# Stacking rotary tiles through a DRAM scratch, thin column tiles for small matmuls, and new engine orders between the MLP and the adapters of an adaLN block

## The chip, the cores and the metric

The kernel runs on one core of a Trainium2 chip. The metric is the device time of one execution in microseconds, as the median of several runs.

## The reference

The block takes x of 4 batch entries ("rows" below) by 512 positions by 256 features, all float32, and a condition vector for each row from which shifts, scales and gates are made.

```python
h = _layernorm(x) * (1 + ca) + sa
x = x + ga * attn_block(h)          # 32 heads of 8, rotary q and k, causal inside 4 blocks of 128,
                                    # RMS norms, then a gated MLP of 512 hidden features
h = _layernorm(x) * (1 + cb) + sb
x = x + gb * ffn_block(h)
# ffn_block: base = silu(h Wg) * (h Wu) @ Wd with 704 hidden features; a router over 8 experts
# (softmax, top 2) weights low-rank adapters of rank 16 on Wg, Wu and Wd, scaled by 2
```

Rotary positions: `x * cos + rot(x) * sin`. Accuracy near float32 is needed.

## The kernel before

Features lie on the 128 partitions and the 512 positions of a row along the free dimension. The four rows are worked one after another in a loop (three turns of `row_steps` and one last copy of it). Each engine runs its own list, written by hand, and waits on semaphores that count the steps of the others. Projections that need accuracy are made of three matmuls on a high and a low part of each operand (`product`, L1259 to L1261); the high part is a rounded copy made on ScalarE, the low part is the difference, made on VectorE.

A row runs through these stages: attention in eight units (2 halves of the heads by 4 blocks), output projection, MLP, then the front of the next row (`front_projections`) woven together with the second norm (`rest`) of this row, then router, adapters and feed-forward. The order of the front on the tensor engine (`front_projections`, L1328 on) is: four q/k projections (`project_qk`), the swap matmuls of the rotary step (`swap`, L1303), the mean and the mean of squares of `rest` (L1276, L1285), the spread of its reciprocal deviation (L1293) and the v projection (`project_v`, L1323 to L1325). Then come the router logits (L1501), the adapters' inner products `ag` and `au`, `base(0)`, transposed picks (L1537), `base(1)`, two more picks, `lora(0, 1)`, `down(0, 0)` and `lora(0, 2)` (L1565 to L1567).

Rotary tiles are four: 0 and 1 are q and k of the first half of the heads, 2 and 3 those of the second. For each tile ScalarE copies the projection out of PSUM (`copy_qk`, L666), GpSimd multiplies it by the cosine (`rope_cos`, L496, into the one buffer `q_cos`, so that it waits for the addition of the tile before), VectorE multiplies the swapped tile by the sine and adds (`rope_sin` L955, `rope_add` L961), ScalarE makes the high part (`rope_high`, L670) and VectorE the low part (`rope_low`, L966). The tile is then stacked: `stack_tile` (L378 to L392) copies three parts of four groups of 32 partitions into `q_st` or `k_st`, 12 DMAs a tile, SBUF to SBUF; SyncE issues tiles 0 to 2, GpSimd tile 3. `highs_back` (L442) copies the high parts into `q_high` and `k_high`, which are the buffers `n_hi` and `n_lo` of the projections, so it waits until those are read; that is four DMAs a tile.

Ahead of the loop SyncE runs `stack(0, 0)`, waits for the v projection and runs `highs_back`. GpSimd's `first_units` then spreads keys (`spread_keys`, L510), after waits for all weight chunks (`chunk_lo`), the rotary low parts and the keys' high parts. The weight chunks are split by ScalarE (`chunk_highs`, L631) and VectorE (`chunk_lows`, L906); three of six are split ahead of the first front and three behind it.

At the start of the feed-forward ScalarE runs `gate_silu(0)`, `copy_pick(0)`, `copy_pick(1)` (L805), and then the high parts of the adapters' inputs (L820); VectorE makes the picks (L1147 to L1156), `ff_product(0)` (L1191), `lora_input` (L1163) and `lora_low` (L1168). `product_high` (L801) writes into the buffers of the rotary high and low parts, so it waits for `half_stacked`.

Of the kernel before, what the change touches and what calls it, by code (L numbers as in the profile page):

```python
# [32 lines left out]
P = 128  # L33
# [122 lines left out]
def adaln_kernel(nc, x, smalls, wmod, wsplit, wplain, consts, masks, out):  # L156
    with ExitStack() as ctx:
# [41 lines left out]
        pool_mark = sb("pool_mark", [P, 1])  # L199
# [30 lines left out]
        qk_sb, q_cos, roped = tile_f[:, 0:2, :], tile_f[:, 2, :], tile_f[:, 4:6, :]  # L230
# [11 lines left out]
        lora_tmp = [tile_f[:, i, :] for i in (4, 6, 10, 11)]  # L242
# [40 lines left out]
        stacked = [signal(f"stacked{i}", PARTS * GQ * 16) for i in range(4)]  # L283
        v_proj = signal("v_proj", 2)
        v_copied = signal("v_copied", 2)
        high_back = [signal(f"high_back{i}", GQ * 16) for i in range(4)]
# [87 lines left out]
        def half_stacked(engine, row, half, ahead):  # L374

            for i in (2 * half, 2 * half + 1):
                engine.wait_ge(stacked[i].sem, stacked[i].count(row, PARTS * GQ * 16, ahead))

        def stack_tile(engine, row, i, ahead):

            half, is_k = i // 2, i % 2
            engine.wait_ge(rope_hi.sem, rope_hi.count(row, i + 1, ahead))
            engine.wait_ge(rope_lo.sem, rope_lo.count(row, i + 1, ahead))
            if engine is nc.gpsimd:

                nc.gpsimd.tensor_tensor(pool_mark[:], con("one"), con("one"), ALU.mult)
            hi, lo = rope_hl[i]
            dest = k_st if is_k else q_st
            for part, src in enumerate((hi, lo, hi) if is_k else (hi, hi, lo)):
                for gq in range(GQ):  # L390
                    engine.dma_start(dest[32 * part:32 * part + 32, half * GQ + gq, :].bitcast(F32),  # L391
                                     src[32 * gq:32 * gq + 32, :].bitcast(F32)).then_inc(stacked[i].sem, 16)  # L392
# [5 lines left out]
        def _(sp):  # L398
# [30 lines left out]
            def stack(row, ahead):  # L429
                for i in range(3):  # L430
                    stack_tile(sp, row, i, ahead)

            def highs_back(i, row, ahead):

                half, is_k = i // 2, i % 2
                dest, stack_of = (k_high, k_st) if is_k else (q_high, q_st)
                for gq in range(GQ):
                    if ahead:
                        src = stack_of[0:32, half * GQ + gq, :]
                    else:  # L440
                        src = rope_hl[i][0][32 * gq:32 * gq + 32, :]
                    sp.dma_start(dest[32 * gq:32 * gq + 32, half, :].bitcast(F32), src.bitcast(F32))\  # L442
                        .then_inc(high_back[i].sem, 16)

            def row_steps(row, last):
# [6 lines left out]
                half_stacked(sp, row, 1, 0)  # L452
                sp.wait_ge(high_back[2].sem, high_back[2].count(row, GQ * 16))
                load(x_res, row, res_loaded)
                if not last:
                    stack(row, 1)

                    for half in range(2):
                        half_stacked(sp, row, half, 1)
# [8 lines left out]
            stack(0, 0)  # L468
            sp.wait_ge(v_proj.sem, v_proj.count(0, 2))
            for i in range(4):  # L470
                sp.wait_ge(rope_hi.sem, rope_hi.count(0, i + 1))
                highs_back(i, 0, 0)
            with sp.Fori(0, B - 1) as row:
                row_steps(row, False)
# [5 lines left out]
        def _(pool):  # L480
# [9 lines left out]
            def rope_cos(row, i, ahead):  # L490

                pool.wait_ge(qk_copied.sem, qk_copied.count(row, i + 1, ahead))
                if i:

                    pool.wait_ge(rope_done.sem, rope_done.count(row, i, ahead))
                nc.gpsimd.tensor_tensor(q_cos, qk_sb[:, i % 2, :], con("cos"), ALU.mult).then_inc(cos_done.sem, 1)  # L496

            def spread_keys(row, u, ahead):

                blk, half = u % BLOCKS, u // BLOCKS  # L500
                if u in (0, BLOCKS):

                    tile = high_back[2 * half + 1]
                    pool.wait_ge(tile.sem, tile.count(row, GQ * 16, ahead))
# [55 lines left out]
            def row_steps(row, last):  # L560
# [21 lines left out]
                if not last:  # L582
                    rope_cos(row, 0, 1)
# [1154 lines left out]
```

## Time and profile before

| | |
|---|---|
| median of 3 runs | 754.75 us (754.65 to 755.93) |
| the profiled execution | 749.13 us |
| its span on the engines | 747.3 us |
| PE busy | 649.1 us (87%) |
| DVE, ACT, POOL busy | 410.6, 321.7, 224.9 us |
| start-up, until the first score matmul | 77.36 us |

In the profile PE is the tensor engine's matmuls and PEld its weight loads, DVE is VectorE, ACT ScalarE, POOL GpSimd and SP SyncE; a q behind the name is the engine's queue, which issues DMAs. L12 is line 12 of the kernel. "Idle before" is the time for which the engine stood before a group, with what released it.

### The profile page before, as it was taken

What the parts mean: (1) busy time and instruction counts of PE and PEld (TensorE: products, weight loads), DVE (VectorE), ACT (ScalarE), POOL (GpSimd) and SP (SyncE); (2) the same over time, 40 slices, a digit from 0 to 9 for tenths busy, and PEclk for the clock granted to TensorE, in tenths of its full rate; (3) what the DMA queues carried; (4) which work ended last, traced back from release to release, by engine and by line L of the source; (5) the groups of instructions that cost most, each with busy time, mean ns of one, the idle gap of its engine ahead of it and who ended that gap; (6) DMA issues with size and microseconds to landing.
All of it is one profiled execution on the core that took longest, in us unless ns stands there. A gap on an engine that the chain in (4) does not pass through costs nothing.

```text
span 747.3 us, 12089 instructions
## 1 busy us (share of the span) xinstructions
PE 649.1 (87%) x4536; PEld 441.6 (59%) x4536; DVE 410.6 (55%) x617; ACT 321.7 (43%) x472; POOL 224.9 (30%) x292
## 2 busy tenths in 40 slices
PE   3770799899999899999999899999999899868996
PEld 2750355667785466657785466657785466637673
DVE  1553456367746564368646564368646564436544
ACT  3332245636544246526534246525533444414442
POOL 3023576204201476115001476115001674010000
PEclk9995799999999899999998799999999899977998
DMA  8245120002302100003202110003202100000000
GB/s 334 71 144 144 33 59 1 2 0 72 99 1 56 61 28 2 1 0 98 72 1 57 51 36 2 1 1 96 73 1 56 57 2 2 1 0 1 0 1 28
DMA packets 16466, 32.62 MB, mean 44 GB/s; under 512 B 5280, under 2 KB 5920, under 8 KB 16160
## 3 DMA queue, kind: packets, MB, share of 16 engines
q1 hardware_dynamic: 14880, 28.74, 12.8%
q0 software_dynamic: 1536, 3.15, 1.5%
q8 instruction: 40, 0.66, 0.4%
q14 instruction: 10, 0.08, 0.0%
HBM read 12.99 MB, written 2.10 MB: 20 GB/s over the span
## 4 chain that ended last, share of the span: by engine, by line
PE 64%; issue 13%; DVE 8%; ACT 7%; SPq 4%; POOL 2%; DMA 1%; DVEq 0%; POOLq 0%; ACTq 0%
PE bank L1424 7%; PE bank L1359 7%; PE bank L1259 7%; PE bank L1260 6%; PE bank L1261 6%; PE bank L1376 3%; PE bank L1402 3%; SPq L391 3%; PE bank L1565 3%; PE bank L1567 3%; PE bank L1566 2%; PE bank L1386 2%; PE bank L1456 2%; ACT tile_f L735 2%; ACT arena L636 2%
## 5 line engine op out<-in xcount | busy, mean ns | idle before, releaser
L1000 DVE TENSOR_REDUCE arena<-bank 128x8 f32<-128x1024 f32 x64 | 77.9, 1223 | 80.8 <-PE bank L1376 80.6
L1359 PE MATMUL bank<-mask 128*128 128x512 bf16 x256 | 83.5, 410 | 29.5 <-POOL k_wide L510 26.2
L1191 DVE TENSOR_TENSOR arena<-arena,bank 128x512 f32<-128x512 f32 (+1 forms) x72 | 49.1, 687 | 82.1 <-ACT arena L785 81.6
L1259 PE MATMUL bank<-n_hi,w_lo 128*128 128x512 f32 x200 | 86.4, 432 | 8.4 <-DVE n_lo L1055 6.0
L785 ACT ACTIVATE arena<-bank 128x512 f32<-128x512 f32 (+1 forms) x72 | 42.5, 596 | 102.1 <-PE bank L1567 53.5
L1260 PE MATMUL bank<-n_lo,w_hi 128*128 128x512 f32 x200 | 80.3, 401 | 0.0
L1261 PE MATMUL bank<-n_hi,w_hi 128*128 128x512 f32 x200 | 80.1, 401 | 0.0
L510 POOL TENSOR_TENSOR k_wide<-n_lo,head_of 128x512 fp32r<-128x512 f32 x32 | 33.1, 1039 | 153.1 <-PE bank L1567 139.4
L735 ACT ACTIVATE tile_f<-bank 128x1024 f32<-128x1024 f32 x64 | 64.2, 1023 | 33.5 <-PE bank L1402 33.4
L719 ACT CAST q_st<-bank 4x512 fp32r<-4x512 f32 x32 | 18.5, 579 | 115.4 <-PE bank L1386 115.4
L530 POOL TENSOR_SCALAR arena_r<-q_st,const 100x512 fp32r<-100x512 f32 x96 | 64.9, 693 | 0.2
L1424 PE MATMUL bank<-tile_f,v_ex 128*32 128x128 f32 x1024 | 52.9, 275 | 2.5 <-ACT tile_f L735 2.5
L1402 PE MATMUL bank<-arena_r,k_st 100*128 100x512 f32 x128 | 54.5, 508 | 0.0
L1176 DVE TENSOR_TENSOR arena_r<-arena,arena_r 128x512 fp32r<-128x512 f32 (+1 forms) x72 | 52.0, 725 | 4.0 <-ACT arena_r L801 3.2
L1359 PEld LDWEIGHTS bank<-mask 128*128 128x128 bf16 x256 | 18.1, 103 | 59.5 <-issue 52.9
L1424 PE MATMUL bank<-tile_f,ones_ex 128*32 128x128 f32 x1024 | 52.3, 273 | 0.0
L1259 PEld LDWEIGHTS bank<-n_hi,w_lo 128*128 128x128 f32 x200 | 38.5, 193 | 22.8 <-DVE n_lo L1055 10.5
L1021 DVE RECIPROCAL arena<-bank 128x128 f32<-128x128 f32 x32 | 30.6, 957 | 37.0 <-PE bank L1424 37.0
L527 POOL TENSOR_TENSOR arena_r<-q_st,const 100x512 fp32r<-100x512 f32 x32 | 33.3, 1041 | 53.4 <-ACT q_st L719 53.4
L801 ACT CAST arena_r<-arena 128x512 fp32r<-128x512 f32 (+1 forms) x72 | 44.1, 613 | 7.5 <-PE bank L1261 4.8
L1260 PEld LDWEIGHTS bank<-n_lo,w_hi 128*128 128x128 f32 x200 | 38.6, 193 | 9.6 <-issue 1.9
L1261 PEld LDWEIGHTS bank<-n_hi,w_hi 128*128 128x128 f32 x200 | 38.4, 192 | 9.5
(158 smaller groups left out, 1263.0 us busy)
## 6 DMA issues: line engine op xcount, KB each, us to landing
q_st<-arena_r SPq DMA_DIRECT2D x96, 64.0 KB, 2.0
k_st<-arena_r SPq DMA_DIRECT2D x48, 64.0 KB, 2.5
k_st<-arena_r POOLq DMA_DIRECT2D x48, 64.0 KB, 2.5
h_next<-in_x SPq DMA_DIRECT2D x4, 512.0 KB, 3.3
tile_f<-in_x SPq DMA_DIRECT2D x4, 512.0 KB, 4.3
out<-arena SPq DMA_DIRECT2D x4, 512.0 KB, 2.6
arena<-in_wmod SPq DMA_DIRECT2D x1, 1536.0 KB, 10.1
n_hi<-q_st SPq DMA_DIRECT2D x24, 64.0 KB, 2.0
```

Source lines behind the costliest of these rows:

```text
L530: last = nc.gpsimd.tensor_scalar(q_ex[u % 2][0:KS, :, hh, :], src, con("head")[0:KS, hh:hh + 1], 1.0, ALU.mult, ALU.mult)
L735: nc.scalar.activation(prob[a], slot(("s2", n)).rearrange("p a s -> p (a s)"), ACT.Exp, scale=SCALE).then_inc(exp_done.sem, 1)
L801: nc.scalar.copy(ff_hl[j % 4][0][0:width], pair_tmp[j % 2][0:width]).then_inc(ff_hi.sem, 1)
L1000: nc.vector.tensor_reduce(neg_max[:, 2 * a:2 * a + 2, MROW:KS], slot(("s1", n)).rearrange("p a (h s) -> p a h s", s=P), AX_X, ALU.max, neg ...
L1176: nc.vector.tensor_tensor(to, pair_tmp[j % 2][0:width], ff_hl[j % 4][0][0:width].bitcast(F32), ALU.subtract)\
L1191: nc.vector.tensor_tensor(pair_tmp[n % 2][0:width], silu_out[n % 2][0:width], up, ALU.mult)\
L1259: nc.tensor.matmul(to, wl[rows, w_cols], ah[rows], start=start, stop=False)
L1260: nc.tensor.matmul(to, wh[rows, w_cols], al[rows], start=False, stop=False)
L1261: return nc.tensor.matmul(to, wh[rows, w_cols], ah[rows], start=False, stop=stop)
L1359: nc.tensor.matmul(to, mask[:, 0, :], mask[:, which:which + 1, :].broadcast_to([P, GH, P]), start=True, stop=False)
L1402: last = nc.tensor.matmul(to[:, g, :], k_st[0:KS, half * GQ + gq, blk * P:(blk + 1) * P], q_ex[u % 2][0:KS, gq], start=False, stop=True)
L1424: last = nc.tensor.matmul(tile, weights, prob[a][:, at:at + P], start=a == j == kind == 0, stop=a == j == 1, skip_group_check=True)
```

## The change

1. Rotary tiles go through a DRAM tensor `rope_tiles`. `keep` writes high and low part of a tile there (2 DMAs of 256 KB); `stack` reads three parts into the stack (2 DMAs); `highs_back` reads the high part from it (1 DMA in place of 4). All are issued by SyncE; GpSimd issues none. Waits on the freeing of the high and low buffers become `half_kept`.
2. Ahead of the loop, the order on SyncE is keep 0 and 1, wait for the v projection, highs 0 and 1, stack 0 and 1, and then the second half.
3. `q_cos` becomes two buffers. In the row loop the additions of tiles 2 and 3 move on VectorE to a place behind the picks and ahead of `ff_product(0)`; their high parts on ScalarE behind `gate_silu(0)` and ahead of the pick copies; their low parts to GpSimd.
4. New orders on the tensor engine and ScalarE in the front: the fourth q/k projection ahead of the mean of squares, swaps 2 and 3 behind the first half of the v projection, the second `copy_qk` ahead of the squares.
5. The mean of squares and the router logits are made with four matmuls of 32 columns each where there was one of 128 ("thin column tiles").

```diff
-        pool_mark = sb("pool_mark", [P, 1])
+        scratch = nc.dram_tensor("rope_tiles", (4, 2, 32, GQ * S), F32).ap()
-        qk_sb, q_cos, roped = tile_f[:, 0:2, :], tile_f[:, 2, :], tile_f[:, 4:6, :]
+        qk_sb, q_cos, roped = tile_f[:, 0:2, :], tile_f[:, 2:4, :], tile_f[:, 4:6, :]
...
+            def keep(i, row, ahead):
+                for part, ready in enumerate((rope_hi, rope_lo)):
+                    sp.wait_ge(ready.sem, ready.count(row, i + 1, ahead))
+                    sp.dma_start(scratch[i, part].rearrange("r (g s) -> g r s", g=GQ), rope_hl[i][part].bitcast(F32))\
+                        .then_inc(kept[i].sem, 16)
+            def stack(i, row, ahead):
...
+                sp.wait_ge(kept[i].sem, kept[i].count(row, 2 * 16, ahead))
...
+                sp.dma_start(dest[0:64], two).then_inc(stacked[i].sem, 16)
+                sp.dma_start(dest[64:MROW], high if is_k else low).then_inc(stacked[i].sem, 16)
+            def stack_all(row, ahead):
+                keep(0, row, ahead)
+                for i in range(1, 4):
+                    keep(i, row, ahead)
+                    stack(i - 1, row, ahead)
+                stack(3, row, ahead)
...
-            stack(0, 0)
+            keep(0, 0, 0)
+            keep(1, 0, 0)
             sp.wait_ge(v_proj.sem, v_proj.count(0, 2))
-            for i in range(4):
-                sp.wait_ge(rope_hi.sem, rope_hi.count(0, i + 1))
+            for i in range(2):
                 highs_back(i, 0, 0)
+            for i in range(2):
+                stack(i, 0, 0)
...
             def rope_cos(row, i, ahead):
...
-                if i:
-                    pool.wait_ge(rope_done.sem, rope_done.count(row, i, ahead))
+                if i >= 2:
+                    pool.wait_ge(rope_done.sem, rope_done.count(row, i - 1, ahead))
...
-                    for i in range(1, 4):
-                        rope_cos(row, i, 1)
-                    stack_tile(nc.gpsimd, row, 3, 1)
+                    rope_cos(row, 2, 1)
+                    rope_cos(row, 3, 1)
+                    rope_low(row, 2, 1)
+                    rope_low(row, 3, 1)
...
                 copy_qk(row, 0, ahead)
+                copy_qk(row, 1, ahead)
                 if ahead:
                     nc.scalar.preload_act_table(ACT.Sqrt)
                     act.wait_ge(rest.centred.sem, rest.centred.count(row, 1))
                     squares(rest, 1, xc)
-                copy_qk(row, 1, ahead)
...
                 copy_v(row, 0, ahead)
...
                 copy_v(row, 1, ahead)
+                if not ahead:
+                    rope_high(row, 2, ahead)
+                    rope_high(row, 3, ahead)
...
                         if j % 2 == 0 and not last:
-                            half_stacked(act, row, j // 2, 1)
+                            half_kept(act, row, j // 2, 1)
...
                 gate_silu(0)
+                if not last:
+                    rope_high(row, 2, 1)
+                    rope_high(row, 3, 1)
...
+                if not is_last:
+                    rope_add(row, 2, 1)
+                    rope_add(row, 3, 1)
...
                 for j in range(S // P):
-                    last = nc.tensor.matmul(bank[:, norm.where, j:j + 1], tile_sum[:, j * P:(j + 1) * P],
-                                            con("mean")[:, 0:1], start=True, stop=True)
+                    for c in range(0, P, 32):
+                        last = nc.tensor.matmul(bank[c:c + 32, norm.where, j:j + 1],
+                                                tile_sum[:, j * P + c:j * P + c + 32],
+                                                con("mean")[:, 0:1], start=True, stop=True)
...
                 project_qk(row, 2, ahead)
                 swap(row, 1, ahead)
+                project_qk(row, 3, ahead)
                 if ahead:
                     mean_squares(rest, row, 1, 0)
-                project_qk(row, 3, ahead)
-                swap(row, 2, ahead)
+                project_v(0)
                 if ahead:
                     spread_rstd(rest, row, 1, 0)
-                project_v(0)
+                project_v(1)
+                swap(row, 2, ahead)
                 swap(row, 3, ahead)
-                project_v(1)
+                project_v(2)
+                project_v(3)
```

The router logits are cut into `for c in range(0, P, 32)` in the same way. `project_v` now takes one of four blocks of positions, not a pair of them. In the row loop VectorE's rotary list becomes centre, sin 0, add 0, sin 1, low 0, add 1, inverse, scale, low 1, sin 2, the second norm's low parts, sin 3.

## Rows read from the trace of the kernel before

**Rows 1.** The page: busy time of each engine and its share.

```profile
PE 649.1 (87%) x4536; PEld 441.6 (59%) x4536; DVE 410.6 (55%) x617; ACT 321.7 (43%) x472; POOL 224.9 (30%) x292
```

**Rows 2.** Windows by stage: length, busy us and instructions of PE, PEld, DVE, ACT, POOL.

```profile
46.00:80.00 34.00, 7.65 (x37) 4.17 (x35) 14.84 (x24) 9.58 (x12) 11.23 (x18) 0.63 0.47 122
...
166.00:189.00 23.00, 21.91 (x113) 16.33 (x112) 17.46 (x36) 13.12 (x22) 12.58 (x16) 1.00 0.32 80
...
189.00:202.00 13.00, 11.33 (x54) 8.54 (x53) 10.96 (x19) 9.28 (x17) 1.64 (x4) 1.00 0.40 105
```

**Rows 3.** Timeline, start-up: start us, us, engine, line, what, idle before.

```profile
46.15 7.57 SPq L391 DMA_DIRECT2D q_st<-arena_r  x12
...
61.44 7.51 SPq L391 DMA_DIRECT2D q_st<-arena_r  x12
...
71.93 2.54 SPq L442 DMA_DIRECT2D n_lo<-arena_r  x4
...
76.08 2.03 POOL L510 TENSOR_TENSOR k_wide<-n_lo,head_of 128x512 fp32r<-128x512 f32 x2 [13.77 <-DMA n_lo<-arena_r]
...
77.36 1.01 PE L1359 MATMUL bank<-mask 128*128 128x512 bf16 x2 [26.17 <-POOL k_wide L510]
```

**Rows 4.** Timeline, start-up: rotary tiles, weight chunks.

```profile
44.77 1.29 DVE L966 TENSOR_TENSOR arena_r<-tile_f,arena_r 128x512 fp32r<-128x512 f32 x1 [0.68 <-ACT arena_r L670]
...
54.87 0.69 DVE L966 TENSOR_TENSOR arena_r<-tile_f,arena_r 128x512 fp32r<-128x512 f32 x1 [0.68 <-ACT arena_r L670]
...
55.22 3.70 ACT L631 CAST w_hi<-arena 128x2048 fp32r<-128x2048 f32 x2
...
57.27 4.49 DVE L906 TENSOR_TENSOR w_lo<-arena,w_hi 128x2048 fp32r<-128x2048 f32 x2
...
61.68 1.02 DVE L906 TENSOR_TENSOR w_lo<-tile_f,w_hi 128x832 fp32r<-128x832 f32 x1
```

**Rows 5.** DMA issues: count, KB each, median us from issue to landing.

```profile
h_next<-in_x SPq DMA_DIRECT2D x4, 512.0 KB, 3.3
...
out<-arena SPq DMA_DIRECT2D x4, 512.0 KB, 2.6
...
tile_f<-in_wsplit SPq DMA_DIRECT2D x1, 1024.0 KB, 13.0
```

**Rows 6.** Timeline, PE in row 0's front.

```profile
172.22 1.12 PE L1303 MATMUL bank<-tile_f,const 128*128 128x512 f32 x2 [0.85 <-ACT tile_f L666]
...
175.48 1.02 PE L1303 MATMUL bank<-tile_f,const 128*128 128x512 f32 x2
...
181.24 1.95 PE L1501 MATMUL bank<-w_plain,arena 128*128 128x8 f32 x16
...
197.57 0.50 PE L1565 MATMUL bank<-arena_r,w_lo 128*128 128x512 f32 x1 [0.94 <-DVE arena L1191]
```

**Rows 7.** Timeline, DVE, ACT and POOL in row 0's front and adapters.

```profile
178.12 0.69 DVE L961 TENSOR_TENSOR tile_f<-tile_f 128x512 f32<-128x512 f32 x1
...
188.63 1.28 DVE L1156 TENSOR_TENSOR arena<-pick,l_exp 128x512 f32<-128x512 f32 x2
...
189.41 1.07 ACT L805 COPY arena<-bank 128x512 f32<-128x512 f32 x2
...
190.43 1.28 DVE L1163 TENSOR_TENSOR tile_f<-arena,bank 128x512 f32<-128x512 f32 x2
...
178.84 0.62 ACT L670 CAST arena_r<-tile_f 128x512 fp32r<-128x512 f32 x1 [2.11 <-DVE tile_f L961]
...
178.95 1.28 POOL L496 TENSOR_TENSOR tile_f<-tile_f,const 128x512 f32<-128x512 f32 x1 [2.09 <-DVE tile_f L961]
```

**Rows 8.** Timeline: mean of squares warm and cold, cold router logits, the last row's clock.

```profile
137.02 1.05 PE L1285 MATMUL bank<-const,arena 128*128 128x1 f32 x8
...
669.19 1.87 PE L1285 MATMUL bank<-const,arena 128*128 128x1 f32 x8 [3.90 <-POOL arena L483]
...
675.95 3.58 PE L1501 MATMUL bank<-w_plain,arena 128*128 128x8 f32 x16 [2.25 <-ACT arena L649]
```

**Rows 9.** Windows on L1424, 32-column matmuls: length, PE busy (count), PEld busy (count), clock.

```profile
125.30:125.38 0.08, 0.00 (x0) 0.00 (x0) 1.00 0.00 0
...
125.30:125.42 0.12, 0.03 (x4) 0.04 (x6) 1.00 0.00 0
...
125.30:125.50 0.20, 0.11 (x4) 0.12 (x8) 1.00 0.00 0
```

**Rows 10.** The chain that ended last: start us, us, what, how often.

```profile
135.14 1.95 PE bank L1424 x64
...
137.09 0.98 PE bank L1285 x8
...
172.22 1.12 PE bank L1303 x2
...
173.34 0.80 PE bank L1285 x8
...
175.64 0.86 PE bank L1303 x2
```

More of the change, by code:

```diff
@@ L376, in half_stacked, with half_kept @@
             for i in (2 * half, 2 * half + 1):
[L377 to L392, printed above, removed]
+                engine.wait_ge(stacked[i].sem, stacked[i].count(row, 2 * 16, ahead))
+        def half_kept(engine, row, half, ahead):
+            for i in (2 * half, 2 * half + 1):
+                engine.wait_ge(kept[i].sem, kept[i].count(row, 2 * 16, ahead))
         block = ctx.enter_context(nc.Block())
@@ L503, in spread_keys @@
                     tile = high_back[2 * half + 1]
-                    pool.wait_ge(tile.sem, tile.count(row, GQ * 16, ahead))
+                    pool.wait_ge(tile.sem, tile.count(row, 16, ahead))
                 if u >= 2:
@@ L700, in front_projections @@
                 copy_qk(row, 3, ahead)
-                rope_high(row, 2, ahead)
-                if ahead:
-                    act.wait_ge(x2_ready.sem, x2_ready.count(row, KT))
-                copy_v(row, 0, ahead)
+                rope_high(row, 1, ahead)
                 if ahead:
@@ L818, in row_steps @@
                         act.wait_ge(lora_lo.sem, lora_lo.count(row, 2))
+                        if not last:
+                            act.wait_ge(rope_lo.sem, rope_lo.count(row, 4, 1))
                     act.wait_ge(lora_in.sem, lora_in.count(row, i + 1))
@@ L1369, in scores_for_max @@
                         tile = high_back[2 * half]
-                        pe.wait_ge(tile.sem, tile.count(row, GQ * 16, ahead))
+                        pe.wait_ge(tile.sem, tile.count(row, 16, ahead))
                 to = fill(row, "s1", n)
@@ L1500, in row_steps @@
                     for kt in range(KT):
-                        last = nc.tensor.matmul(bank[:, 3, j * E:(j + 1) * E], xc[:, kt, j * P:(j + 1) * P],
-                                                plain("r")[:, kt * E:(kt + 1) * E], start=kt == 0, stop=kt == KT - 1)
+                        for c in range(0, P, 32):
+                            last = nc.tensor.matmul(bank[c:c + 32, 3, j * E:(j + 1) * E],
+                                                    xc[:, kt, j * P + c:j * P + c + 32],
+                                                    plain("r")[:, kt * E:(kt + 1) * E],
+                                                    start=kt == 0, stop=kt == KT - 1)
                 last.then_inc(route_ready.sem, 1)
```

127 lines of the change are left out of this document (68 added, 59 removed).

## The prediction

> **What bounds the kernel now.** I read the page first: PE is busy for 649.1 of 747.3 us [rows 1], so a row is bound by the tensor engine unless a stage shows otherwise. The windows by stage show which does: in the start-up, from 46 to 80 us, PE works 7.65 of 34 us [rows 2]. The timeline says why. SyncE issues 12 DMAs for each of three rotary tiles without a pause, from 46.15 to 68.95 us (0.63 us each), and only then the copies of the high parts; the keys' copies are issued up to 74.47 and GpSimd, idle for 13.77 us, starts the first keys at 76.08. PE stood for 26.17 us and starts at 77.36 [rows 3]. All else that GpSimd waits for is ready when VectorE ends the last weight chunk, at 62.70 [rows 4].
>
> In the loop the front of row 0 (166 to 189 us) has PE busy for 21.91 of 23 us; the start of the adapters (189 to 202) 11.33 of 13, with VectorE at 10.96 [rows 2]. So the front is bound by PE with one stop, 0.85 us before the second swap, which waits for ScalarE's copy [rows 6]. In the adapters PE runs into VectorE: `lora(0, 2)` stands 0.94 us for the product of L1191 [rows 6], and VectorE has hardly a gap there.
>
> **Part 1, start-up.** The old SyncE list in front of the first keys is 36 stack DMAs and 8 high ones. The new one is 4 keeps and 2 highs. Tile 1's low part, about 48.7 us, is kept about 2.6 us after its issue (the 512 KB store to DRAM took 2.6 us [rows 5], these are half of it), the v projection ends near 50.7, and the highs of tile 1 are issued by 52 and landed after some 3.3 us (the 512 KB load [rows 5]): by about 55. Both stacks are issued by 54.5 and land by 58, and they are first needed several us after the first scores.
>
> What is late next is VectorE's chunk work, 62.70. It is tied to ScalarE's chunk copies, which begin at 55.22 behind the last v copy, behind the last rotary high part [rows 4]. The rotary list gets shorter: the cosine has two buffers (it stood 2.09 us for the addition [rows 7]), and the two last low parts (0.69 to 1.29 us each [rows 4]) leave VectorE for GpSimd. Working the lists through with those durations (sine 0.68, addition 0.69, high part 0.62) the fourth addition ends at 51.4, not 54.2, the high parts at 52.4, and the chunks end at 59.9. GpSimd's two low parts (1.28 each, by its cosine [rows 7]) end at 54.4, under that. Start of the keys: 59.9 in place of 76.08, so **-16.2 us**. Bounds: if the chunk work doesn't move, -13.4; if the chip gives the mean of squares back too (part 3), -17.5. The cover is wide: the round trip through DRAM may take 5 us longer before it shows.
>
> **Part 2, the front and the adapters, three rows.** In the front, `copy_qk(1)` now goes ahead of the squares, so the stop of 0.85 us goes, and with it some 0.25 us of weight load and swap that were not covered (the chain has 1.12 us for that swap and 0.86 for the third [rows 10]). The four-block order of v changes no work. What was hidden stays hidden: the sum of squares is ready on GpSimd when the fourth q/k projection ends (173.0 against 173.5 by the lists), though it now stands behind two cosines. Front: -1.1 us.
>
> Behind it VectorE is the engine to follow: its list between the second norm's low parts and the picks is as long as before (one sine in place of one low part, 0.68 each), so the picks end at 189.91 - 1.1 = 188.8. Now come the moved steps: two additions, 0.69 each less overlap, 1.3 together, to 190.1. ScalarE, which used to copy the picks at 189.41 [rows 7], stands for these additions: high part 2, high part 3 at 190.1 to 190.7, then the first pick copy to 191.3. So `lora_input(0)` begins at 191.3, where it began at 190.43 [rows 7]: 0.9 us late. Queued behind it on ScalarE and VectorE are all the adapters' high and low parts, `ff_product(1)` and `(2)`, and for these PE waits already; so `lora(0, 2)` comes at 198.4, not 197.57. PE gives back all it won in the front: **+0.9 us a row, +2.6 for three.** Bounds: -1.1 a row if the moved steps find cover, +1.9 if the front gives nothing. The low parts on GpSimd run until about 193.2, before ScalarE's wait for them at its third adapter input (194 or later). The keep of tile 3 is issued at about 193.8, lands near 197, and `product_high(2)` wants it near 200.5. The 12 DMAs of GpSimd a row vanish from a queue that had time.
>
> The copies of the high parts in the loop wait, as before, for the last `base`; four DMAs in place of 16 end earlier, but the keys still wait for the last adapter matmul. Nothing.
>
> **Part 3, thin columns.** There are 16 means of squares: 13 warm ones at about 0.9 us (0.80 and 0.98 in the chain [rows 10]; 1.05 recorded, with the pipeline's end [rows 8]) and 3 at half the clock at 1.87 [rows 8], two of them in the start-up; and four router products, 1.95 [rows 6] for three and 3.58 for the last [rows 8]. The records show 8 and 16 pieces, so each matmul is two passes, and each passes at about the time its 128 weight columns take to load. Thin ones would be 32 and 64 passes of a quarter of the columns. What does such a pass cost? The kernel has them in L1424. Its windows begin empty at 125.38; by 125.42 four matmuls and six loads have started, by 125.50 no fifth matmul [rows 9]. So the four column quarters load and run beside each other, some 8 ns apart, and the fifth waits for the 128 streamed columns of the first, of which the thin ones have 1 or 8. I estimate 60 ns for a round of four (four loads and four matmuls at 8 ns): 8 rounds make 0.5 us, 16 rounds 1.0, and 0.1 to 0.2 more where the array changes over. So 0.65 in place of 0.9, and at half the clock 1.2 in place of 1.87 and 2.2 in place of 3.58. The upper bound is L1424's own rate, 1.95 us for 64 [rows 10], 0.98 for 32, which is no gain; the lower one load-bound rounds of 27 ns, 0.2 and 0.45 us.
>
> Path: of the 13 warm ones I count 10 (those inside attention, where PE waits now and then, by half), -2.5; the router products of rows 0 to 2 nothing, since VectorE's list starts from the v projection and decides there; the last row's mean -0.7 and router -1.4, as there each engine waits for the one before (PE stood 3.90 and 2.25 us before them [rows 8]); the second mean of the start-up -0.7. **-5.3 us.**
>
> The Trainium skill (TensorEngine Tiling (Array Packing), Performance Considerations and Key Properties) speaks against this part: it gives each matmul about 60 cycles of overhead, so that one column costs as much as 60, and says that a change of tiling mode drains the array. By it, as an estimate, 32 passes are 32 x 25 ns = 0.8 us at full clock plus two drains, so no gain or a loss. The four starts within 40 ns [rows 9] say that this overhead isn't paid one after the other between quarters, which the page's own independent tiles allow; for streams of one column no row shows it.
>
> GpSimd beside VectorE is a cost too: a low part took 1.29 us with GpSimd's cosine beside it and 0.69 without [rows 4]. The Trainium skill (GPSIMD Engine Reference, on the shared SBUF interfaces) names this contention for VectorE instructions with two SBUF inputs; the trace agrees, 1.29 against 0.69. In the adapters GpSimd's two low parts may stretch one `lora_low` by 0.6 us; this is in the bound of part 2.
>
> **Sum.** -16.2 + 2.6 - 5.3 = -18.9 us. Span 747.3 - 18.9 = 728.4; the profiled execution had 1.8 us around its span and lay 5.6 us under the median, so 728.4 + 1.8 + 5.6 = 735.8: **736 us**.
>
> **Rivals.** (a) Thin tiles bring nothing or lose: then part 3 is 0 to +3 (16 groups with 0.2 us of change-over), the time 741 to 744. For it: L1424's rate and the rule above; against it the four starts. Chance 0.2. (b) The moved steps find cover or the thin tiles give the lower bound: rows at -1.1, 6 us less, about 730. For it: only 0.9 us of delay a row carries the loss, and the low bound of a thin pass is far below my value; against it the old stop of 0.94 us at `lora(0, 2)` [rows 6], where nothing covers a delay. Chance 0.13. (c) Something else holds the start-up, as the first stack or a chunk copy at some 66 us, where only 10 us come back: 742. Chance 0.07. (d) Slower than before: the place is ScalarE's `product_high(2)` in the three loop turns, which now waits for tile 3's store to DRAM. It has about 6.7 us from issue; a landing of L us costs L - 6.7 a row. It decides against the change from L = 13, as then three rows cost 19 us. For it: a load of the crowded start took 13.0 us [rows 5]; against it 2.6 us for stores in an idle loop [rows 5]. Chance 0.03. (e) The change doesn't do what it says, the SyncE list still being long in front of the keys (a DMA of 256 KB to DRAM taking several times the 0.6 us of issue): about 754, no change. Chance 0.02. The forecast has 0.55.
>
> **How the numbers follow.** The range goes from 729, (b) with a little of its bounds, to 743, which takes in (c) and most of (a). A difference of 0.2% (1.5 us) is what a measurement can tell: faster 0.95, same 0.015, slower 0.035.
>
> **What would show it.** The first keys (L510) at 59 to 61 us and the first score matmul at 61 to 62; GpSimd released there by VectorE's last chunk, not a DMA. The second swap without a stop; `lora(0, 1)` and `lora(0, 2)` each with a stop of 1 us or more, the picks' copies right behind two high parts. The 32 passes of L1285's line at 0.5 to 0.7 us. Wrong it would be if GpSimd's first keys came after 65 us, if the stops in the adapters were as short as before, or if ScalarE stood for a landing store.

## The result and the profile after

The changed kernel takes 813.87 us (median of 5, 810.36 to 814.68), the kernel before 754.65 in the same comparison (5 runs): a ratio of 1.081, 95% interval 1.0752 to 1.0867. That is 59 us slower, where I had forecast 19 us faster. The profiled execution took 810.36 us with a span of 808.4. A ratio compares the faster of two states that the runs of a kernel fall into, so it can differ a little from the quotient of the medians.

The page of the changed kernel, called after from here on: busy time, the packets of one instruction queue, the chain's shares, and two groups of DMA issues (count, KB each, median us to landing). A keep is the store of one part of a rotary tile to DRAM, a stack read its way back into the stack, a high copy the read of the high part.

```profile
PE 649.4 (80%) x5112; PEld 433.0 (54%) x5112; DVE 404.8 (50%) x609; ACT 323.2 (40%) x472; POOL 209.9 (26%) x248
...
q14 instruction: 19, 0.16, 0.1%
...
PE 52%; issue 13%; DMA 12%; DVE 9%; ACT 6%; SPq 4%; POOL 2%; POOLq 0%; DVEq 0%; ACTq 0%
...
k_st<-rope_tiles SPq DMA_DIRECT2D x8, 512.0 KB, 6.8
...
k_st<-rope_tiles SPq DMA_DIRECT2D x8, 256.0 KB, 14.3
```

PE is busy as long as before (649.4 against 649.1 us [rows 1]); its share fell from 87 to 80% because the span grew. The chain has 12% on DMA and 4% on SyncE's queue, 9% of the span on the keeps alone. So the new time is in the transfers through DRAM. The waits of after say who stands for them (us in all, times, longest):

```profile
PE bank L1291 <- DVE arena_r L1208: 38.9, 4, 13.2
ACT arena_r L825 <- DMA rope_tiles<-arena_r: 36.4, 3, 12.5
PE bank L1395 <- POOL k_wide L532: 28.5, 2, 16.3
POOL k_wide L532 <- DMA n_lo<-rope_tiles: 25.5, 2, 14.3
POOL arena_r L549 <- DMA k_st<-rope_tiles: 14.2, 1, 14.2
DVE mod L1036 <- issue: 10.5, 2, 5.2
```

There are three places. First, ScalarE stands some 12 us in each of three rows (12.5 at most) at L825, `product_high(2)`, for tile 3's store to DRAM, and PE behind it through VectorE. Second, GpSimd stands in the start-up for the copies of the high parts and for a stack. Third, VectorE stands 5.2 us twice with nothing to wait for ("issue"). Of these only GpSimd's wait for the keys' copies has a counterpart in the trace of before, one of 13.77 us [rows 3]; there ScalarE waits for no store and VectorE has no such stop.

The start-up in the timeline of after (start, us, engine, line, idle before), and two pieces of the chain in the same stretch, with the keep of row 0's adapters behind them:

```profile
62.77 2.04 POOL L532 TENSOR_TENSOR k_wide<-n_lo,head_of 128x512 fp32r<-128x512 f32 x2 [11.27 <-DMA n_lo<-rope_tiles]
...
64.06 1.01 PE L1395 MATMUL bank<-mask 128*128 128x512 bf16 x2 [16.28 <-POOL k_wide L532]
...
109.70 1.04 POOL L532 TENSOR_TENSOR k_wide<-n_lo,head_of 128x512 fp32r<-128x512 f32 x1 [14.25 <-DMA n_lo<-rope_tiles]
```

```profile
46.34 9.62 DMA rope_tiles<-arena_r
...
59.93 16.12 SPq L424
...
76.10 13.18 DMA rope_tiles<-arena_r
...
89.30 20.25 DMA n_lo<-rope_tiles
...
207.17 17.10 DMA rope_tiles<-arena_r
```

A keep of 256 KB lands 9.6, 13.2 and 17.1 us after its issue, a copy of high parts 20.3. SyncE's queue itself stands: one issue at 59.93 took 16.12 us, where the others take 0.54. PE's first score starts at 64.06, 13.3 us before that of before [rows 3], and yet the row loses it all again: the fifth of GpSimd's key operations comes only at 109.70.

Why are they slow? Windows of after: length, busy us of five engines, granted clock, DMA share, GB/s. In the first two the keeps are under way (a high copy is queued behind them in the second). In the third stack reads and the keys' high copy are under way, and only two engines are at work.

```profile
46.50:50.50 4.00, 1.28 (x11) 1.08 (x10) 3.72 (x8) 2.47 (x4) 1.50 (x2) 1.00 0.26 99
52.00:55.50 3.50, 0.00 (x0) 0.00 (x0) 3.36 (x6) 2.14 (x2) 0.00 (x0) 0.50 0.26 99
104.00:109.00 5.00, 0.00 (x0) 0.00 (x0) 0.00 (x0) 0.00 (x0) 0.00 (x0) 0.50 0.13 50
```

0.26 of 16 engines is 4, and 0.13 is 2, at some 25 GB/s each. The keep's DRAM side is `"r (g s) -> g r s"`, whose outermost size is 4; the first stack transfer's is 2. The Trainium skill (DMA: Bandwidth & Descriptors, Why a DMA increments its semaphore by 16 and not by 1) states it: a transfer goes to the largest number of engines, up to 16, that divides the slowest dimension of both sides. The trace agrees, with 4.2 and 2.1 engines' worth of busy time.

The rows add up so. The table has the start of the first probability-times-v matmul and of the router's matmul in each row, and PE's last instruction, from the timelines (us).

| kernel | row 0 pv, router | row 1 | row 2 | row 3 | last |
|---|---|---|---|---|---|
| before | 91.7, 181.2 | 257.6, 347.2 | 425.9, 515.5 | 591.8, 676.0 | 739.9 |
| after | 89.2, 191.5 | 291.2, 378.9 | 476.6, 564.3 | 657.4, 739.0 | 801.0 |

Row 0 up to the router loses 10.2 us, the three steps from router to router 21.5, 17.1 and 14.2, and the rest gains 2.0: 61.1. In the first of these steps PE's first score matmul of the next row comes 77.1 us behind the router (60.2 before), so 16.9 us go where ScalarE stands for the store. Another 6.5 go between scores and pv, where VectorE has one of its 5.2 us stops; the rest of the row is 1.8 shorter. A part of the 16.9 is the clock: PE came out of the wait at L825 at half of it.

```profile
225.77 0.80 PE bank L1291
226.57 0.43 PE bank L1292
...
231.69 0.38 PE bank L1292
...
232.31 0.23 PE bank L1291
```

These are pieces of the chain: after 13 us of idling nearly every matmul takes 0.43 us until 231.7, then 0.23. That is 6.2 us at half the clock; behind the other two stops it is 3.7 and 6.2 us. Over the span the mean granted clock is 0.903, before it was 0.943. With two levels, 1.2 and 2.4 GHz, that is 2 x (1 - 0.903) x 808.4 = 157 us at the lower one against 85, and 72 us more of it cost up to 36, less what of it PE stood idle. So a stop is paid once as idle time and in part again as a slow stretch behind it.

### The profile page after: what moved, and what is told of

Read it like the earlier page. It is cut to its first block, busy times and chain, and to the rows that moved or that the text cites. A ratio compares the mean times of both kernels' runs of the same rounds, so it can differ in the third digit from the quotient of the medians.

```text
span 808.4 us, 13046 instructions
## 1 busy us (share of the span) xinstructions
PE 649.4 (80%) x5112; PEld 433.0 (54%) x5112; DVE 404.8 (50%) x609; ACT 323.2 (40%) x472; POOL 209.9 (26%) x248
## 3 DMA queue, kind: packets, MB, share of 16 engines
q1 hardware_dynamic: 13168, 40.26, 15.8%
## 4 chain that ended last, share of the span: by engine, by line
PE 52%; issue 13%; DMA 12%; DVE 9%; ACT 6%; SPq 4%; POOL 2%; POOLq 0%; DVEq 0%; ACTq 0%
DMA rope_tiles<-arena_r 9%; PE bank L1460 6%; PE bank L1395 6%; PE bank L1291 6%; PE bank L1292 5%; PE bank L1293 5%; PE bank L1412 3%; SPq L424 3%; DMA n_lo<-rope_tiles 3%; PE bank L1438 2%; PE bank L1604 2%; PE bank L1606 2%; PE bank L1605 2%; PE bank L1422 2%; PE bank L1492 2%
## 5 line engine op out<-in xcount | busy, mean ns | idle before, releaser
L1395 PE MATMUL bank<-mask 128*128 128x512 bf16 x256 | 87.4, 427 | 40.0 <-POOL k_wide L532 28.5
L1291 PE MATMUL bank<-n_hi,w_lo 128*128 128x512 f32 x200 | 89.6, 448 | 11.2 <-DVE n_lo L1084 6.0
L1292 PE MATMUL bank<-n_lo,w_hi 128*128 128x512 f32 x200 | 82.2, 411 | 0.0
L1291 PE MATMUL bank<-arena_r,w_lo 128*128 128x512 f32 x80 | 33.6, 420 | 39.2 <-DVE arena_r L1208 38.9
L825 ACT CAST arena_r<-arena 128x512 fp32r<-128x512 f32 (+1 forms) x72 | 44.1, 613 | 44.0 <-DMA rope_tiles<-arena_r 36.4
L1438 PE MATMUL bank<-arena_r,k_st 100*128 100x512 f32 x128 | 56.2, 522 | 0.0
L1604 PE MATMUL bank<-arena_r,w_lo 128*128 128x512 f32 (+1 forms) x96 | 38.9, 405 | 8.7 <-DVE arena_r L1200 4.8
## 6 DMA issues: line engine op xcount, KB each, us to landing
k_st<-rope_tiles SPq DMA_DIRECT2D x8, 256.0 KB, 14.3
```

The lines of the kernel that those rows point to most:

```text
L1291: nc.tensor.matmul(to, wl[rows, w_cols], ah[rows], start=start, stop=False)
L1292: nc.tensor.matmul(to, wh[rows, w_cols], al[rows], start=False, stop=False)
L1395: nc.tensor.matmul(to, mask[:, 0, :], mask[:, which:which + 1, :].broadcast_to([P, GH, P]), start=True, stop=False)
L1438: last = nc.tensor.matmul(to[:, g, :], k_st[0:KS, half * GQ + gq, blk * P:(blk + 1) * P], q_ex[u % 2][0:KS, gq], start=False, stop=True)
L1604: nc.tensor.matmul(to, wl[:, cols], ah, start=False, stop=False, skip_group_check=True)
```

## The experiments

Each number is against the kernel before on the same chip. Medians, with the ratio where there were several runs; e2, e3, e6 and e7 have one run each.

**e1: the same transfers, cut so that 16 divides the slowest dimension.**

```diff
-        scratch = nc.dram_tensor("rope_tiles", (4, 2, 32, GQ * S), F32).ap()
+        scratch = nc.dram_tensor("rope_tiles", (4, 2, P, S), F32).ap()
-                    sp.dma_start(scratch[i, part].rearrange("r (g s) -> g r s", g=GQ), rope_hl[i][part].bitcast(F32))\
+                    sp.dma_start(scratch[i, part], rope_hl[i][part].bitcast(F32))\
-                sp.dma_start(dest[0:64], two).then_inc(stacked[i].sem, 16)
-                sp.dma_start(dest[64:MROW], high if is_k else low).then_inc(stacked[i].sem, 16)
+                for n, part in enumerate((0, 1, 0) if is_k else (0, 0, 1)):
+                    sp.dma_start(dest[32 * n:32 * n + 32], scratch[i, part].rearrange("(g r) s -> r g s", g=GQ))\
```

> The changed kernel with the scratch laid out as 128 rows of 2 KB a part, so that keep and highs_back have 128 rows on both sides, and the stack read by three DMAs of 32 partitions, not by one of 64 and one of 32. The bytes, the round trip through DRAM and all other lists are those of the changed kernel. Theory A (its DMAs use 4 and 2 of the 16 DMA engines, since their outer dimensions are 4 groups and 2 parts: 99 GB/s at a DMA share of 0.26 and 50 GB/s at 0.13 in its trace): landings fall from 6 to 22 us to 3 to 4 us, GpSimd has no stop at L532 for a DMA behind the first keys, ScalarE none at product_high(2), and the time is 725 to 740 us. Rival B (a trip through DRAM, with the write confirmed before the read may start, is slow as such): landings stay above 6 us and the time stays above 790 us. Rival C (SyncE's issue is the bound: 16 us in one instruction at L424): with eight more issues a row no gain, 810 us or more.

743.20 us (10 runs), ratio 0.9884 (0.9836 to 0.9932). Against after's ratio of 1.081 that is 0.093 of 754.65, 70 us. Rivals B and C are out. The time still lies above the 725 to 740 of theory A, for a reason that e5 shows. Its keep lands in 2.0 us in the median; the first keys, a window with these transfers, and VectorE in the first loop jump:

```profile
rope_tiles<-arena_r SPq DMA_DIRECT2D x32, 256.0 KB, 2.0
```

```profile
59.06 2.04 POOL L531 TENSOR_TENSOR k_wide<-n_lo,head_of 128x512 fp32r<-128x512 f32 x2 [6.72 <-DVE w_lo L935]
...
60.35 1.01 PE L1394 MATMUL bank<-mask 128*128 128x512 bf16 x2 [11.72 <-POOL k_wide L531]
...
240.75 0.17 DVE L1035 COPY mod<-mod_all 128x12 f32 x1 [5.10 <-issue]
...
243.46 1.09 PE L1421 MATMUL bank<-const,arena 128*100 128x128 f32 x4 [6.99 <-DVE arena L1028]
```

```profile
54.00:58.00 4.00, 0.00 (x0) 0.00 (x0) 4.00 (x3) 0.97 (x2) 0.00 (x0) 0.50 1.06 224
```

The first keys start at 59.06, released by VectorE's last chunk: the forecast was 59.9 and this releaser. In the window all 16 engines are at work (share 1.06), on keeps, reads and copies mixed; at 224 GB/s that is 14 GB/s an engine, where after's four moved 25 each, so four times the engines gave 2.3 times the rate. No engine waits for a transfer of `rope_tiles` any more. What stays is a stop that the transfers have nothing to do with: VectorE stands 5.1 us at L1035, the first operation behind the loop's jump, and PE 6.99 us behind it, where before it stood at most 3.0 us for the maxima that VectorE makes there. The lead over the kernel before is 15.8 us at row 0's router (165.4 for 181.2) and 8.2 at the next row's pv (249.4 for 257.6).

**e2 and e3: one half of that repair each.** e2 cuts keeps and high copies into four transfers of 32 partitions and leaves the stacks; e3 has e1's three stack transfers and leaves keeps and highs at four engines.

```diff
-                    sp.dma_start(scratch[i, part].rearrange("r (g s) -> g r s", g=GQ), rope_hl[i][part].bitcast(F32))\
+                    for g in range(GQ):
+                        sp.dma_start(scratch[i, part][:, g * S:(g + 1) * S],
+                                     rope_hl[i][part][32 * g:32 * g + 32].bitcast(F32)).then_inc(kept[i].sem, 16)
```

> The changed kernel with keep and highs_back cut into four DMAs of 32 partitions each, the stack reads left as they are (one of 64 partitions whose DRAM side is two parts, one of 32). Theory A: keeps land in 3 to 4 us where no stack read is under way, but the 512 KB reads stay on 2 engines (10.5 us each at 50 GB/s), and the keeps' shares on these engines queue behind them: the first keys at 60 us, a long stop in the second half of row 0's attention as before, ScalarE's stop at product_high(2) still 5 us or more; 780 to 800 us. Rival B: no difference to the changed kernel but for more issues, 812 us or more.

> The changed kernel with the stack read by three DMAs of 32 partitions, keep and highs_back left as they are (outer dimension 4). Theory A: the stack lands in 4 to 5 us, a pair of keeps takes 512 KB at 99 GB/s, 5.3 us and a fixed part; so the stops of row 0's attention shrink to under 8 us in all (32 us in the changed kernel) and ScalarE's stop at product_high(2) from 12.5 to about 2 to 4 us a row: 745 to 765 us. Rival B: 805 us or more.

One run each: 789.23 (expected 780 to 800) and 774.04 us (expected 745 to 765). So slow keeps and highs alone (e3) cost some 31 us over e1, slow stacks alone (e2) 46, and the sum of 77 is near the 70 of both. Both keep the DRAM layout of after and change only how a transfer is cut, so the layout is not the cause. Their waits (e2, then e3):

```profile
ACT arena_r L826 <- DMA rope_tiles<-arena_r: 18.2, 3, 6.6
POOL arena_r L550 <- DMA k_st<-rope_tiles: 15.2, 1, 15.2
POOL k_wide L533 <- DMA n_lo<-rope_tiles: 13.1, 1, 13.1
```

```profile
ACT arena_r L824 <- DMA rope_tiles<-arena_r: 18.6, 3, 6.4
POOL k_wide L531 <- DMA n_lo<-rope_tiles: 15.3, 2, 13.0
```

The keep of row 0's adapters in the chain of e3:

```profile
186.85 12.17 DMA rope_tiles<-arena_r
```

Either half leaves ScalarE's stop at half the size of after's 12.5 and GpSimd's in the start-up at nearly its full size, 13 to 15 us. In e2 the keeps are cut for all engines and still wait. The median landing of its `rope_tiles` transfers is 2.0 us, but the chain has a keep issued at 59.84 that took 18.39 us and one of row 0's adapters at 205.00 that took 8.94. Each was issued right behind stack reads on two engines, so I put the wait down to these: a transfer on few engines slows the next ones. Part of e2's 6.6 us is also that its last keep goes out later, after eight issues of 0.43 us in place of two.

**e4: thin tiles alone in the kernel before.**

```diff
-                    last = nc.tensor.matmul(bank[:, norm.where, j:j + 1], tile_sum[:, j * P:(j + 1) * P],
-                                            con("mean")[:, 0:1], start=True, stop=True)
+                    for c in range(0, P, 32):
+                        last = nc.tensor.matmul(bank[c:c + 32, norm.where, j:j + 1],
+                                                tile_sum[:, j * P + c:j * P + c + 32],
+                                                con("mean")[:, 0:1], start=True, stop=True)
```

The router's matmuls are cut the same way.

> The kernel before with the thin column tiles alone (mean of squares and router logits in quarters of 32 columns). In the changed kernel's trace 32 thin passes take 0.43 us and 64 take 0.72 us warm, 0.65 us for 32 at half the clock, against 0.80 to 0.98, 1.81 and 1.88 before. Theory T: on its path lie 13 warm ones (0.4 us each, those inside attention by half), the last row's router and mean (2.3 and 1.2 us) and the start-up's second mean (1.2 us): 7 to 9 us less than before, a ratio of 0.988 to 0.991. Rival U (in the loop the adapters' chain on VectorE swallows them): 3 to 5 us less, 0.993 to 0.996.

745.13 us (10 runs), ratio 0.9924 (0.9871 to 0.9976): 5.7 us faster by the ratio, with an interval from 1.8 to 9.7. That lies between theory T (7 to 9) and rival U (3 to 5), and the interval takes in both. The rows of after for the same passes, a mean of squares and a router product at full clock:

```profile
184.66 0.43 PE L1318 MATMUL bank<-const,arena 128*32 128x1 f32 x32
...
191.48 0.72 PE L1538 MATMUL bank<-w_plain,arena 128*32 128x8 f32 x64
```

**e5 to e7: shift VectorE's program.** e1 with 8, 48 or 100 one-column clears of an unused tile on VectorE at its start, nothing else.

```diff
             nc.vector.memset(eps_col[:], EPS).then_inc(zeroed.sem, 1)
+            for i in range(8):
+                nc.vector.memset(spare[:, i:i + 1], 0.0)
```

> e1_all16 with eight one-column memsets on VectorE right at its start, at 1 us, where VectorE idles until 8.8 us; nothing else. In e1_all16's trace VectorE stands 5.1 us without a releaser at L1035, the first instruction of the loop's body, at both taken jumps back, and PE's scores stand behind it; in the kernel before this is not there. Theory P (the place of the loop in VectorE's instruction stream decides whether the jump's target has to be loaded again; the change made the part ahead of the loop shorter): a shift of 8 instructions may or may not move the loop over the edge of a block; if it does the two stops go and the time is 10 us less, 732 to 736 us; if not, the same 743. Rival Q (the stop belongs to the changed body or to the DMAs running then): 743 whatever the shift.

> As e5_pad8 with 48 memsets. Theory P: at one at least of the three shifts (8, 48, 100) the two stops of 5.1 us at L1035 are gone, and stops may come up elsewhere. Rival Q: two stops of 5.1 us in each of the three.

> As e5_pad8 with 100 memsets (some 3 to 6 us of VectorE's idle time at the start). Theory P and rival Q as for e6_pad48.

e5: 730.89 us (5 runs), ratio 0.9715 (0.9664 to 0.9766). e6 and e7, one run each: 730.85 and 731.49. Eight more instructions make it 12 us faster, and the intervals of e1 and e5 don't touch. VectorE's first jump in e5, and the same instruction queue on its page:

```profile
234.76 0.62 DVE L1038 COPY mod<-mod_all 128x12 f32 x1
235.30 2.34 DVE L1031 TENSOR_REDUCE arena<-bank 128x8 f32<-128x1024 f32 x2
```

```profile
q14 instruction: 9, 0.07, 0.0%
```

The stop of 5.10 us is gone, and the instruction queue has 9 packets for 19. All kernels with the stop (after, e1, e2, e3, e8) have 19; all without it (before, e4, e5 to e7, e9 to e12) have 9 or 10. The Trainium skill (Runtime: NRT & Kernel Launch, Instruction fetch mechanics) offers the reason: instructions are fetched in blocks of 256, an engine holds two, and a taken branch to outside them waits for a fetch. The trace agrees in what it can show, the stop at the jump, the packets, and that 8 more instructions in front of the loop end it; how the blocks lie it doesn't show. The change took eight VectorE instructions away (617 before [rows 1], 609 after), the low parts that went to GpSimd. Only two of these stood ahead of the loop; the other six are two in each of its three turns. So the clears don't restore the old place of the loop, they only move it.

**e8 and e9: the moved steps put back.** e1 (e8) and e5 (e9) with the last two rotary additions and high parts in their places of before.

```diff
                 rope_sin(row, 2, 1)
+                rope_add(row, 2, 1)
                 n_lows(rest, row, 1, 0)
                 rope_sin(row, 3, 1)
+                rope_add(row, 3, 1)
```

> e1_all16 with the moved steps of the row loop put back: on VectorE the additions of tiles 2 and 3 right behind their sines, on ScalarE the high parts of tiles 2 and 3 behind the v copies, none behind gate_silu(0). GpSimd keeps the two low parts. Theory M (the moved steps delay the picks' copies, and PE pays it at lora(0, 2); in e1_all16 the two products of L1222 begin 0.9 us later against the row's start than before): the adapters' part of a row is 1.5 to 2.5 us shorter than in e1_all16, 5 to 7 us in all, if VectorE's two stops of 5.1 us at the loop's head stay as they are. Rival N (the additions only change places, the front gets as much longer): within 1 us a row.

> The 32-row scratch layout and the thin tiles, with the moved steps of the row loop put back in their places of before and eight one-column clears added on VectorE at the start. Theory: e8 (the same without the clears) carried VectorE's two stops of 5.0 us at the loop's back-jump, so they go here: 740.5 - 10 = 730.5, and against e5 (730.9) the difference is what the moves are worth, +0.9 in each of three rows less about 1.1 of the front, so 729 to 731 here. Rival: e5 owes its time to the moves, and this kernel stays near e8 at 737 to 741. Shown by VectorE's idle time before the loop's first operation in the waits.

e8: 740.46 us (4 runs), ratio 0.9875 (0.9794 to 0.9956), with the stop of 5.0 us twice; that is 2.7 us under e1 and not the 5 to 7 of theory M. e9: 728.48 us (4 runs), ratio 0.9675 (0.96 to 0.975), the fastest median of all. e8 to e9 is the shift again, 12 us. e5 to e9, the moves, is 2.4 us, within the intervals; by the two traces the three steps from router to router take 490.84 us with the moves and 489.42 without. The moves bring nothing that can be measured. Nor is theory M's place right: from the router to `lora(0, 2)` row 1 takes 18.8 us without the moves (e9) and 18.1 with them (e5).

**e10: e5 without thin tiles.** **e11: after with the 8 clears.** **e12: before with the 8 clears.**

> The 32-row scratch layout, the moved steps and the eight clears, with the mean-of-squares and router matmuls at 128 columns wide again, as before. Theory: the thin tiles are worth here what e4 measured alone (5.7 us by its ratio), so 730.9 + 5.7 = 736.6, range 734 to 739. Rival: part of e4's gain came from something else, and this one is within 2 us of e5, at 729 to 733.

> The changed kernel with nothing but the eight clears on VectorE at the start added: the slow transfers stay. Theory: VectorE's two stops of 5.2 us end on the path there too, and adding the clears takes about 10 us: 804, range 801 to 808. Rival: the waits for the slow transfers hide the stops, and the time stays at 811 to 815.

> The kernel before with the eight clears at the start. The trace of before has no such stop on VectorE, so the theory expects no change, 753 to 756. Rival: the clears help by something other than the stop, and this kernel gains several us as well, 744 to 750. Or the shift brings a stop about, and it loses about 10 us.

e10: 744.05 us (4 runs), ratio 0.9864 (0.9817 to 0.9911), above both the 734 to 739 of the theory and the rival's 729 to 733. By the medians the thin tiles are worth 13 us in the repaired kernel, by the ratios 11 with an interval of some 6 to 16. That is more than the 5.7 of e4, but the two intervals overlap. The two profiled executions lie further apart, by 17.3 us of span, since e5's is its fastest run. Some 4 us of that are in the start-up (first scores at 59.2 for 63.0), where 1.1 us is the input's later landing. Most of the rest goes with the clock (e5, then e10):

```profile
core 0: 724.7 us, clock 0.960
```

```profile
core 0: 742.0 us, clock 0.940
```

By the formula above that is 58 us at the lower level against 89, up to 15 us of time. The windows some 62 us behind row 1's router (at 329.7 us in e5, at 338.2 in e10) show where (e5, then e10; the granted clock is the third number from the right):

```profile
392.00:396.00 4.00, 3.39 (x11) 1.16 (x10) 3.79 (x5) 0.00 (x0) 0.00 (x0) 1.00 0.01 4
396.00:400.00 4.00, 2.47 (x12) 1.05 (x12) 2.31 (x5) 0.58 (x1) 1.46 (x2) 1.00 0.34 134
```

```profile
400.00:404.00 4.00, 4.00 (x10) 1.31 (x10) 3.40 (x5) 0.00 (x0) 0.00 (x0) 0.57 0.02 4
404.00:408.00 4.00, 4.00 (x12) 1.79 (x10) 1.52 (x3) 0.36 (x1) 0.00 (x0) 0.58 0.01 4
```

e10 falls to the lower clock between two rows, e5 doesn't there, although PE was busy for 2.8 us of the 4 before in both. All four runs of e10 had a clock of 0.936 to 0.940, all five of e5 0.949 to 0.960. Why the thin tiles keep it up is not shown; e4, with the same tiles on the old start-up, had 0.935 to 0.956, so they alone don't.

e11: 803.10 us (4 runs), ratio 1.0645 (1.059 to 1.07), as expected. The stop was worth 0.0165 of 754.65, 12 us, in the changed kernel too. It is 49 us over the kernel before, and 0.093 over e5, the same kernel with its transfers cut for 16 engines: 70 us again. e12: 753.31 us (10 runs), ratio 0.9951 (0.991 to 0.9991). Where there is no stop the clears bring little: the median is 1.7 us under its partner's (755.01), the ratio 3.7 us with an interval that ends just under 1, against 12 us where there is one. The ratio leans on one run of 743.96, 6 us under the next, and the kernel before itself runs from 743.3 to 756.5 over the comparisons. Whether anything is left to explain is open.

## Why the prediction was wrong, point by point

**The step that failed: "kept about 2.6 us after its issue", "landed after some 3.3 us", "both stacks ... land by 58".** I priced the new transfers by their size, from rows of other transfers whose both sides have 128 partitions outermost [rows 5], and took half the size for half the time. The new ones have 4 and 2 outermost and ran on 4 and 2 engines: 9.6 to 17.1 us for a keep, up to 20.3 for a high copy, 14.3 for a stack of 256 KB in the median. With the same bytes cut for 16 engines (e1) the keep took 2.0 us in the median. "The round trip through DRAM may take 5 us longer before it shows" was about the right margin, and it was passed: the keys' high copy landed near 62.7 and not by 55, and the first keys came at 62.77 and not at 59.9. This step alone is worth 70 us, by e1 against after and by e5 against e11.

**Rival (d) was the right mechanism with the wrong chance.** It named the place (ScalarE's `product_high(2)`), the price (L - 6.7 a row) and the point from which it decides (13 us). The keep took 17.1 us: the formula gives 10.4, ScalarE stood 12.5. The other 2 us are in the 6.7: the keep went out only 4.7 us before ScalarE wanted it, since SyncE stood 3.2 us issuing two stack reads ahead of it. In e3 a keep of 12.2 us gives 5.5, and it stood 6.4. As a price of the row the formula also leaves out what follows: PE runs at half the clock for 4 to 6 us behind each stop. I gave it 0.03 because "2.6 us for stores in an idle loop" spoke against it, which is the failed step again. I also took it for a fault of the loop alone, though "if ScalarE stood for a landing store" stood among the signs of being wrong. The start-up had the same fault in another place, (c) in my list, where a stack and the highs of row 0 came late, and waits of 14.2 and 14.3 us took back the gain of the first keys.

**The stop behind the jump was in no rival.** VectorE stood 5.2 us twice, and it is worth 12 us with what hangs on it. The trace of before couldn't show it. The sum took VectorE's jump as free because it was free there.

**Part 1 came out by luck.** In e1 the first keys start at 59.06 (59.9 forecast), the first score at 60.35, 17.0 us earlier than before (16.2 forecast), released by the chunks and not by a DMA. But e1 has the thin columns, and e10 has not. There the last chunk ends at 61.55 (59.9 forecast, 62.70 before), the keys start at 61.68 and the first score at 62.97, 14.4 us earlier than before. The rotary additions end at 52.5 (51.4 forecast, 54.2 before), and VectorE's work on the condition's columns behind them took 3.7 us in place of 1.8, part of it beside GpSimd's low parts. So the chunks moved by 1.1 us and not by 2.8; the prediction had priced these low parts for GpSimd alone. One of those column steps, in e10 and in the kernel before:

```profile
52.59 1.17 DVE L918 TENSOR_SCALAR mod_all<-mod_all 128x8 f32<-128x8 f32 x1
```

```profile
55.69 0.17 DVE L886 TENSOR_SCALAR mod_all<-mod_all 128x8 f32<-128x8 f32 x1
```

The thin columns made up for it: 2.7 us in the start-up (59.2 for 63.0, less 1.1 for the input), where part 3 had 0.7.

**Part 2 was right in size; its cause is not shown.** From the mean of `rest` to `lora(0, 2)` row 0 takes 29.6 us before (167.99 to 197.57), and 30.5 in e1 (153.05 to 183.51) and in e10 with wide tiles (156.84 to 187.29): +0.9 us, as forecast. But with the moved steps put back (e9) the same stretch takes 31.2 us in row 1, so it is not simply their delay. In after PE stands 1.59 us in front of the adapter matmul `lora(0, 1)`, and 0.97 at `lora(0, 2)`, where it stood for 0.94 [rows 6]; the second swap has no stop.

**Part 3 was near in the path's sum and too careful in the pass.** I forecast 0.65 for a mean, 1.0 for a router product; they took 0.43 and 0.72, which is 13 and 11 ns a pass. At the lower clock the mean took 0.60 for 1.2 and the router 1.04 for 2.2. Together PE was busy 10.7 us with the two lines, where it was 27.7 before. The e4 gain of 5.7 us stands against -5.3, but within an interval of 1.8 to 9.7, and e10 gives 11. The Trainium skill's rule of some 60 cycles a matmul (TensorEngine Tiling (Array Packing), Performance Considerations), which spoke against, would be 25 ns a pass; here passes followed each other faster. What the clock gives on top in e10 I didn't see.

**The sum.** -18.9 of the parts, +70 for the transfers' engines, +12 for the jump: 63 us slower by that, 59 measured. With both undone, e5 has 730.9 and e9 728.5, where I had forecast 736 for the change; so the parts are worth 21 to 25 us together, by the ratios of e5 and e9, and not 18.9. The prediction also held that a measurement can tell 1.5 us. The intervals above are 3 to 6 us wide to either side, and one kernel's runs spread over 10 us.

## What to carry to other kernels

Read the outermost dimension of both sides of a transfer before its size: a layout that is handy for the copy behind it may leave 12 of 16 engines idle, and it can delay those queued after it. When a store frees a buffer, write down who takes that buffer next and how long a landing that place bears, and price the landing by a transfer of the same shape. Where an edit adds or takes instructions in or ahead of a hardware loop, look in the new trace for idle time with no releaser at the first operation behind the jump, and try a few instructions of padding.

## What the runs showed of the hardware that I had not expected

- A transfer whose slowest dimension is 4 moved 99 GB/s, one with 2 moved 50, beside 224 with 16 engines busy [the window of e1]. One issue stood 16.12 us on SyncE while earlier transfers were under way.
- The jump back in a loop cost VectorE 5.0 to 5.2 us, both times, or nothing: eight more instructions ahead of the loop made the difference.
- Matmuls of 32 weight columns and 1 streamed column followed each other every 13 ns.
- Thin tiles were worth 5.7 us (1.8 to 9.7) in one kernel and 11 (6 to 16) in another, where the granted clock went from 0.936 to 0.940 up to 0.949 to 0.960 with them.
